# A two-block vision tower, image pairs in one merged order: the next image's patches, first attention and routing move beside the current image's second attention

## The chip, the cores and the metric

One core of a Trainium2 chip runs the whole program. The metric is the time of one execution in device microseconds, from three runs. Engine names are those of the profile: PE (TensorE's matmuls), PEld (its weight loads), DVE (VectorE), ACT (ScalarE), POOL (GpSimd), SP (SyncE, which here issues all DMAs).

## What is computed

64 images of 3 x 224 x 224 go through a patch embedding and two transformer blocks of width 192; an image has 197 tokens.

```
h = patches(x) @ W + b, class token in front, + pos_embed
h = h + softmax(q k^T / sqrt(192)) v          of layernorm(h), one head        "first attention"
h = h + w[e] * (gelu(n @ W1[e] + b1[e]) @ W2[e] + b2[e])   n = layernorm(h), e = argmax of
                                              softmax(mean over tokens of n @ Wg)   "routing", ffn 0
h = h + proj(12 heads of softmax(q k^T / 4) v) of layernorm(h)                 "second attention"
h = h + ffn of layernorm(h)                   191 patch rows: fc1, gelu, fc2   "ffn 1"
                                              6 class rows: routed pairs of five experts
```

The expert of ffn 0 is known only after the first attention of that very image, so its weights are fetched by index while the kernel runs. The six class rows of all images are done together after the loop.

## The kernel before, in words

Images are taken in pairs: p = 0 is called the **even** image here and p = 1 the **odd** one. Tokens lie as 2 tiles of 99 rows. The work on an image is cut into named stages (STAGES, line 69), and each engine has one function `stages(name, p, it)` that issues its own share of a stage and waits by semaphores. `run_stages` (line 405) lets every engine walk the same list, ORDER, once per pair: `merged_order` (line 84) makes it from the letters of MERGE (line 80), where a takes the even image's next stage, b the odd image's next one, r one regrouping step of the patches on POOL. The odd image starts B_FIRST (line 79) stages late, so the stages of one half of it belong to the pair before ("behind"); stages in AHEAD (line 68) are done for the next pair, and are run once before the loop for the first. Every engine works strictly through its share of this list.

The stages are, in the order of one image: `x` (28 transposes of regrouped pixels, for both images, copies by DVE and ACT), `tok0/1` (patch matmuls), `statN/normN/turnN` (layernorm N: moments on DVE, the power on POOL, the scaling on DVE, four transposes on PE, a copy on ACT and two remainders on DVE), `q0 v0 s0 p0 o0` (first attention: folded query-key product, values, scores, transposed weights, output), `route` (sum over tokens on DVE, PE, then seven small DVE operations and one exponential; then the loads of the expert's weights on SP, line 473), `hid0_* out0_*` (ffn 0), `qk1_* v1` (queries, keys, values), `max0` to `max5` (scores of two heads each, whose maxima DVE takes), `maxT` (the maxima turned into rows of the operand stacks by two DMAs, line 507), `att0` to `att13` (scores with the maximum in them, exponentials on ACT; every fourth head the products with the values, then shuffle, reciprocal and product on DVE: a "head group"), `proj`, layernorm 4, `hid1_* out1_*` (ffn 1).

Queries and keys as high and low parts are put into the operand stacks `q_stack` and `k_stack` by eight DMAs per image on SP, after `qk1_0` and `qk1_1`. `k_stack` lies in the tile `shared` (line 171), which at another time holds W1 of the expert. The matmuls stand in helpers: line 640 (`accumulate`), 664 (layernorm transposes), 687 and 689 (`hid_out`), 706 (`x`), 740 (`p0`), 786 (`max`), 792 (`maxT`), 804 and 817 (`att`). On DVE: 943, 948, 955 (layernorm), 965 (`x`), 981 (`turn`), 1014 to 1031 (`route`), 1035 (`out0_1`), 1041 (`qk1`), 1050 (`max`), 1059 to 1063 (head group). Each image has four PSUM banks; TURN_BANK and HIDDEN_BANK (lines 106 and 107) say which stages use which.

In ORDER before, the even image's `max0` to `att2` stand with no stage of the odd image between them; the odd image's `max0` to `att2` have the even image's layernorm 4 and ffn 1 between them. The first attention of each image stands beside the other's late second attention, layernorm 4 and ffn 1, and is followed by routing and, 14 to 16 places later in the merged order, by ffn 0. Layernorm 1 of the next pair is made a pair ahead (`x`, `tok`, layernorm 1 only are in AHEAD).

Of the kernel before, what the change touches and what calls it, by code (L numbers as in the profile page):

```python
# [17 lines left out]
ALU = mybir.AluOpType  # L18
# [6 lines left out]
D = 192  # L25
# [21 lines left out]
RING = 6  # L47
STAGED = 2
# [12 lines left out]
def ffn_stages(n):  # L61
# [6 lines left out]
AHEAD = ["x", "tok0", "tok1"] + norm_stages(1)  # L68
STAGES = (["q0", "v0", "s0", "p0", "o0"] + norm_stages(2)
          + ["route", "x", "tok0", "tok1", "stat1", "split", "norm1", "hid0_0", "hid0_1", "turn1",  # L70
             "hid0_2", "out0_0", "out0_1"] + norm_stages(3) + ["qk1_0", "qk1_1", "qk1_2", "v1"]
          + [("max", j) for j in range(HEADS // 2)] + ["maxT"] + [("att", s) for s in range(HEADS + 2)]
          + ["proj"] + norm_stages(4) + ffn_stages(1))

B_FIRST = 38
MERGE = ("bbbbbabbabbbbabbababbbabaababbbababaaabbaaabababararbaabrbabbbaabrbbarabbrbaaaaa"  # L80
         "aaabaababaaaabaababaaabaaabbabbrabbabaabbab")
# [24 lines left out]
TURN_BANK = {1: 3, 2: 3, 3: 0, 4: 1}  # L106
# [3 lines left out]
def vit_kernel(nc, x, tok_w, tok_b, cls_tok, pos, attn_w, wg, w1, b1, w2, b2, w_qkv, w_proj, b_proj,  # L110
               fc1_w, fc1_b, fc2_w, fc2_b, gate_pair, atom_in_w, atom_in_b, atom_out_w, atom_out_b,
               balance, out, scratch):
    with ExitStack() as ctx:
# [52 lines left out]
        with ExitStack() as loop:  # L166
# [13 lines left out]
            w2_sb = two("w2_sb", [128, HC, D])  # L180
# [50 lines left out]
            probs0 = [probs[p][0][:, 0, :, :] for p in range(2)]  # L231
            turned = [probs[p][0][:, 1, :, :] for p in range(2)]
            y = two("y", [R, T, D])
# [164 lines left out]
        def norm_count(n, it):  # L398

            if n == 1:  # L400
                return 1 if isinstance(it, int) and it == 0 else 4 * it - 1
            last = isinstance(it, int) and it == PAIRS - 1
            return 4 * it + {2: 2, 3: 4 - last, 4: 5 - last}[n]
# [27 lines left out]
        def _(sp):  # L431
# [36 lines left out]
            def stages(name, p, it):  # L468
# [4 lines left out]
                if name == "route":  # L473

                    sp.wait_ge(expert_ready[p], it + 1)
# [44 lines left out]
                if name == "out1_1":  # L520
# [3 lines left out]
                                 y[p][NCLS - 1:R - 1, 0, :]).then_inc(stored[p], 16)  # L524
                    sp.dma_start(out[bass.ds(img, 1), R:SEQ].rearrange("o s d -> (o s) d"),
                                 y[p][0:R - 1, 1, :]).then_inc(stored[p], 16)
# [66 lines left out]
        def _(pe):  # L593
# [82 lines left out]
            def hidden(p, n, j, chunk):  # L676
                for c in (2 * j, 2 * j + 1):
                    last = accumulate(bank[p][HIDDEN_BANK[n][j]][:, (c % 2) * SP_:(c % 2 + 1) * SP_],
                                      swapped(products(tokens(p), chunk(c))))
                last.then_inc(hid_done[p], 1)  # L680
# [585 lines left out]
```

## Time and profile before

| | us |
|---|---|
| runs | 4169.99, 4172.8, 4182.94 (median 4172.8) |
| the profiled execution | 4169.49 |
| its span, first to last instruction | 4167.7 |
| PE busy | 3189.7 |
| DVE busy | 2134.8 |
| ACT busy | 1402.9 |
| POOL busy | 360.5 |

The mean granted clock of TensorE over the span is 0.862. The loop over pairs starts at some 67 us and PE leaves it at 4044 us; behind it come the class rows. An instruction row of the trace gives its start in us from the span's start, its length, engine, line and operation, output and inputs, shapes, how many were merged, and in brackets how long its engine sat idle before it and what ended that.

### The profile page before, as it was taken

Reading aid. Unit: us, or ns where it says so; the run is one execution under the profiler, and the core shown is the slowest. Engines: PE = TensorE matmul, PEld = TensorE weight load, DVE = VectorE, ACT = ScalarE, POOL = GpSimd, SP = SyncE. Lnnn points to the kernel's source line nnn. Section 1 sums busy time; section 2 is a strip of 40 time slices with the busy share of each in tenths; the row PEclk is TensorE's granted clock in tenths of the full one; section 3 lists DMA queues with packets and bytes.
Section 4 is the critical chain, followed back from the end, with each engine's and each line's share of the span. In section 5 each row is a group of like instructions: output and inputs, shape, how many; then the busy total and the mean of one; then the engine's idle time right before and its main releaser. Section 6 shows DMA issues by size and latency. Waiting matters only on the chain.

```text
span 4167.7 us, 63512 instructions
## 1 busy us (share of the span) xinstructions
PE 3189.7 (77%) x23190; PEld 2834.1 (68%) x23190; DVE 2134.8 (51%) x5288; ACT 1402.9 (34%) x2904; POOL 360.5 (9%) x746
## 2 busy tenths in 40 slices
PE   4777877777877777777777787777778777777757
PEld 3667766767766676776666776667677666677646
DVE  4555555554555555555555455554555555555433
ACT  2333333333333333333333333333333333333321
POOL 1000000010000000010001000010010000100000
PEclk9888888888988888888888898888888888889877
DMA  4332222332322333222233232223322223322221
GB/s 122 79 80 70 69 60 47 81 79 69 79 57 56 64 79 78 71 70 58 47 81 79 69 81 66 55 54 80 80 69 73 56 47 80 79 73 66 64 62 32
DMA packets 127223, 287.54 MB, mean 69 GB/s; under 512 B 28791, under 2 KB 95368, under 8 KB 116173
## 3 DMA queue, kind: packets, MB, share of 16 engines
q1 hardware_dynamic: 127180, 286.97, 29.7%
q8 instruction: 27, 0.44, 0.0%
q14 instruction: 16, 0.12, 0.0%
HBM read 192.23 MB, written 15.00 MB: 50 GB/s over the span
## 4 chain that ended last, share of the span: by engine, by line
PE 47%; DVE 29%; DMA 8%; issue 5%; SPq 4%; ACT 4%; POOL 3%; DVEq 0%; POOLq 0%; ACTq 0%
PE banks L640 21%; PE banks L687 8%; DVE inv L1061 5%; DVE hx L955 5%; PE banks L817 5%; DMA shared<-low 4%; DVE nmax L1050 4%; PE banks L786 4%; PE banks L804 3%; DMA shared<-nmaxT 3%; DVE stats L943 3%; POOL rstd L586 2%; PE banks L664 2%; DVE xnT L981 2%; DVE sums L1059 2%
## 5 line engine op out<-in xcount | busy, mean ns | idle before, releaser
L786 PE MATMUL banks<-shared,q_stack 128*99 128x198 f32 x1536 | 282.2, 336 | 238.4 <-issue 103.3
L1050 DVE TENSOR_REDUCE nmax<-banks 99x4 f32<-99x788 f32 x384 | 360.3, 974 | 155.8 <-PE banks L786 152.5
L786 PEld LDWEIGHTS banks<-shared,q_stack 128*99 128x99 f32 x1536 | 225.3, 225 | 292.3 <-issue 110.8
L640 PE MATMUL banks<-xnT,fc_wT 128*128 128x198 f32 x1920 | 359.3, 363 | 42.1 <-DVE xnT L981 42.1
L640 PEld LDWEIGHTS banks<-xnT,fc_wT 128*128 128x128 f32 x1920 | 346.0, 278 | 50.1 <-DVE xnT L981 50.0
L804 PE MATMUL banks<-q_stack,shared 128*99 128x198 f32 x1536 | 268.0, 301 | 140.1 <-DMA shared<-nmaxT 118.4
L1191 ACT ACTIVATE xnT<-banks 128x396 fp32r<-128x396 f32 x192 | 96.1, 501 | 820.6 <-PE banks L664 820.6
L584 POOL TENSOR_TENSOR var_eps<-moments,eps 99x2 f32<-99x2 f32 x256 | 51.1, 200 | 3642.2 <-DVE moments L948 3642.2
L804 PEld LDWEIGHTS banks<-q_stack,shared 128*99 128x99 f32 x1536 | 204.4, 194 | 203.6 <-DMA shared<-nmaxT 106.8
L687 PE MATMUL banks<-w_sb,hidT 128*99 128x192 f32 x1536 | 338.7, 383 | 0.0
L955 DVE TENSOR_SCALAR hx<-hx,moments,rstd 99x192 f32<-99x192 f32 (+1 forms) x768 | 248.0, 385 | 160.8 <-POOL rstd L586 157.2
L1226 ACT ACTIVATE probs_first<-banks 99x396 f32<-99x396 f32 x256 | 114.0, 497 | 616.2 <-PE banks L804 616.2
L687 PEld LDWEIGHTS banks<-w_sb,hidT 128*99 128x99 f32 x1536 | 293.2, 201 | 11.7
L687 PE MATMUL banks<-fc_wT,hidT 128*99 128x192 f32 x1536 | 273.0, 327 | 0.0
L640 PE MATMUL banks<-tok_wT,xT 128*99 128x192 f32 x1536 | 270.0, 330 | 3.5 <-ACT xT L1182 0.9
L1061 DVE RECIPROCAL inv<-sums 128x198 f32<-128x198 f32 x192 | 267.2, 1392 | 6.6
L817 PE MATMUL banks<-probs_rest,vals 99*32 99x198 f32 (+1 forms) x2048 | 186.7, 361 | 100.4 <-DVE headT L1063 65.5
L640 PEld LDWEIGHTS banks<-tok_wT,xT 128*99 128x99 f32 x1536 | 245.4, 168 | 8.9 <-issue 7.2
L1226 ACT ACTIVATE probs_rest<-banks 99x396 f32<-99x396 f32 x512 | 228.0, 497 | 64.6 <-PE banks L804 61.3
L687 PEld LDWEIGHTS banks<-fc_wT,hidT 128*99 128x99 f32 x1536 | 240.6, 166 | 0.5
L1209 ACT ACTIVATE hidT<-banks,fc_bc 128x198 f32<-128x198 f32 x384 | 142.5, 423 | 290.3 <-PE banks L640 290.3
L664 PE MATMUL banks<-ident,hx 99*128 99x99 f32 x1024 | 158.0, 284 | 106.2 <-DVE hx L955 103.9
(191 smaller groups left out, 5592.3 us busy)
## 6 DMA issues: line engine op xcount, KB each, us to landing
shared<-w_split SPq DMA_DIRECT2D x64, 1188.0 KB
xin<-in_x_dram SPq DMA_DIRECT2D x32, 1176.0 KB
w_sb<-in_L_ffn_W_dram SPq DMA_DIRECT2D x64, 576.0 KB, 6.2
w_last<-w_split SPq DMA_DIRECT2D x64, 384.0 KB
q_stack<-hi SPq DMA_DIRECT2D x128, 148.5 KB
q_stack<-low SPq DMA_DIRECT2D x128, 148.5 KB
shared<-hi SPq DMA_DIRECT2D x128, 148.5 KB
shared<-low SPq DMA_DIRECT2D x128, 148.5 KB
```

What stands on the lines that cost most here:

```text
L640: last = t_.matmul(dst, a, b, start=(j == 0), stop=(j == len(pairs) - 1))
L664: last = t_.transpose(b[:, k * SP_ + t * R:k * SP_ + (t + 1) * R], xn[p][:, t, k * 128:(k + 1) * 128], ident[0:R, 0:R])
L687: t_.matmul(b[0:R, t * D:(t + 1) * D], hidT[p][:, c, t * R:(t + 1) * R], w[:, c, :], start=(c == 0), stop=False)
L786: last = t_.matmul(b[n % 4][0:R, t * SP_:(t + 1) * SP_], q_stack[p][:, n, t * R:(t + 1) * R], k_stack[p][:, n, :], start=True, stop=True)
L804: last = t_.matmul(b[s % 2][0:R, kt * SP_:(kt + 1) * SP_], k_stack[p][:, s, kt * R:(kt + 1) * R], q_stack[p][:, s, :], start=True, stop=True)
L817: last = t_.matmul(b[2][r:r + 32, 0:SP_], vals[p][0:rows, kt, head(h), :], ring(p, h)[0:rows, kt, :], start=(kt == 0), stop=(kt == T - 1))
L943: last = v.bn_stats(stats[p][:, t, :], (h_tok[p] if n == 1 else h_tiles[p])[:, t, :])
L955: last = v.tensor_scalar(xn[p][:, t, at:at + D - lo], (h_tok[p] if n == 1 else h_tiles[p])[:, t, lo:D], moments[p][:, t, 0:1], rstd[p][:, ...
L1050: v.tensor_reduce(nmax1[p][:, :, 2 * j:2 * j + 2].rearrange("p t h -> p h t"), src, AX, ALU.max, negate=True).then_inc(nmax1_ready[p], 1)
L1061: v.reciprocal(inv1[p][:], sums1[p][:]).then_inc(inv1_ready[p], 1)
L1209: last = s_.activation(hidT[p][:, c, :], b[HIDDEN_BANK[layer][j]][:, (c % 2) * SP_:(c % 2 + 1) * SP_], ACT.Gelu, bias=bias[:, c:c + 1], sc ...
L1226: s_.activation(ring(p, s).rearrange("p k s -> p (k s)"), b[s % 2][0:R, 0:T * SP_], ACT.Exp).then_inc(p1_ready[p], 1)
```

## The change

What it does: AHEAD now reaches from `x` to `route` and a new stage `load` (the expert's DMAs, which so far stood in `route`): all of that is done for the next pair. In STAGES the first attention, layernorm 2 and routing of the next image stand between the `att` stages of the same image's second attention (BESIDE says behind which), `x`, `tok` and layernorm 1 stand between layernorm 3 and `v1`, `q0` and `v0` before `max0`, `load` behind `proj`. B_FIRST and MERGE are other values. For this, buffers no longer shared: `vals0`, `probs0` and `turned` get tiles of their own (laid over `w2_sb`'s place, see the diff), the first attention keeps its result in `h_tok`, `y` goes and the output is stored from `h`. Banks: the first attention uses bank 3 (before: 0 to 3) and `v0` bank 1; layernorm 4 turns into `tokT`. `load` waits for `proj` of the image before, whose keys lie in `shared`. The kinds, shapes and numbers of the instructions of each stage stay, but for `p0` and `o0`, which take 98 keys in the second tile where it took 99.

The order after, from one `max0` of the even image to the next (E even, O odd, +1 the next pair's image):

```
E.max0 O.turn4 E.max1 E.max2 O.hid1_0 O.hid1_1 E.max3 O.hid1_2 E.max4 E.max5 O.out1_0 O.out1_1
O.hid0_0 O.hid0_1 E.maxT O.hid0_2 O.out0_0
E.att0 E.s0+1 E.att1 O.out0_1 E.att2 E.p0+1 O.stat3 E.att3 E.att4 E.o0+1 O.norm3 E.stat2+1
E.att5 E.att6 E.att7 O.tok0+1 E.norm2+1 E.att8 O.tok1+1 O.turn3 E.att9 E.att10 E.att11 E.att12 E.turn2+1
O.qk1_0 E.att13 O.qk1_1 O.v1 O.stat1+1 E.route+1 O.norm1+1 E.proj E.load+1 O.turn1+1 E.stat4
O.q0+1 E.norm4 O.v0+1
O.max0 O.max1 E.turn4 O.max2 O.max3 E.hid1_0 O.max4 O.max5 E.hid1_1 O.maxT E.hid1_2 E.out1_0
O.att0 O.s0+1 O.att1 E.out1_1 O.att2 E.hid0_0 O.p0+1 E.hid0_1 E.hid0_2 E.out0_0 E.out0_1 E.stat3
O.att3 O.att4 O.o0+1 E.x+1 O.stat2+1 O.att5 O.att6 O.att7 O.norm2+1 E.norm3 E.tok0+1 O.att8 O.att9
O.att10 E.tok1+1 O.att11 E.turn3 O.att12 O.turn2+1 O.att13
E.qk1_0 E.qk1_1 E.v1 E.stat1+1 O.route+1 E.norm1+1 O.proj O.load+1 E.turn1+1 O.stat4 E.q0+1 E.v0+1 O.norm4
```

The diff, cut to its core:

```diff
-AHEAD = ["x", "tok0", "tok1"] + norm_stages(1)
-STAGES = (["q0", "v0", "s0", "p0", "o0"] + norm_stages(2)
...
+AHEAD = (["x", "tok0", "tok1"] + norm_stages(1) + ["q0", "v0", "s0", "p0", "o0"] + norm_stages(2)
+         + ["route", "load"])
+BESIDE = {0: ["s0"], 2: ["p0"], 4: ["o0", "stat2"], 7: ["norm2"], 12: ["turn2"], 13: ["route"]}
+ATTENTION = []
+for s in range(HEADS + 2):
+    ATTENTION += [("att", s)] + BESIDE.get(s, [])
+STAGES = (ffn_stages(0) + ["stat3", "x", "norm3", "tok0", "tok1", "turn3", "qk1_0", "qk1_1", "v1"]
+          + norm_stages(1) + ["q0", "v0"] + [("max", j) for j in range(HEADS // 2)] + ["maxT"] + ATTENTION
+          + ["proj", "load"] + norm_stages(4) + ffn_stages(1))
...
-B_FIRST = 38
+B_FIRST = 30
...
-TURN_BANK = {1: 3, 2: 3, 3: 0, 4: 1}
+TURN_BANK = {1: 0, 2: 3, 3: 1, 4: 1}
...
-            w2_sb = two("w2_sb", [128, HC, D])
+            w2_sb, vals0, probs0, turned = [], [], [], []
+            for p in range(2):
+                with ExitStack() as weights:
+                    w2_sb.append(sb(f"w2_sb{p}", [128, HC, D], stack=weights))
+                vals0.append(sb(f"vals0{p}", [R, T, D], stack=loop))
+                probs0.append(sb(f"probs0{p}", [R, T, SP_], stack=loop))
+                turned.append(sb(f"turned{p}", [R, T, SP_], stack=loop))
...
-            y = two("y", [R, T, D])
...
+        def norm_source(p, n):
+            return h_tok[p] if n <= 2 else h_tiles[p]
+
+        def turned_tile(p, n):
+            return (xnT if n in (2, 3) else tokT)[p]
...
-                if name == "route":
+                if name == "load":
+                    if not isinstance(it, int) or it:
+                        sp.wait_ge(proj_done[p], it)
+                        sp.nop(nofuse=True)
                     sp.wait_ge(expert_ready[p], it + 1)
...
-                    if not isinstance(it, int) or it:
-                        pe.wait_ge(logit_ready[0], it)
...
                 elif name == "q0":
                     pe.wait_ge(xnT_ready[p], norm_count(1, it))
+                    if not isinstance(it, int) or it:
+                        pe.wait_ge(v_ready[p], 2 * it)
...
                 elif name == "v0":
                     if not isinstance(it, int) or it:
-                        pe.wait_ge(out_ready[p], it)
-                    values(p, it, b[3], attn_wv, tokT)
+                        pe.wait_ge(low_ready[p], 2 * it - 1)
+                    values(p, it, b[1], attn_wv, tokT)
...
-                        if not (isinstance(it, int) and it == PAIRS - 1):
-                            pe.wait_ge(xnT_ready[p], norm_count(1, it + 1))
+                        if isinstance(it, int) and it == 0:
+                            pe.wait_ge(logit_ready[p], 1)
+                        else:
+                            pe.wait_ge(out_ready[p], it)
...
-                        pe.wait_ge(v_ready[p], 2 * it + 2)
+                        if isinstance(it, int) and it == PAIRS - 1:
+                            pe.wait_ge(v_ready[p], 2 * it + 2)
+                        else:
+                            pe.wait_ge(v_ready[p], 2 * it + 3)
+                            pe.wait_ge(g_ready[p], it + 2)
...
+                    if name == "out1_0" and not (isinstance(it, int) and it == PAIRS - 1):
+                        pe.wait_ge(logit_ready[p], it + 2)
...
+                if not (n == 1 and isinstance(it, int) and it == 0):
+                    dve.wait_ge(xn_turned[p], norm_count(n, it) - 1)
...
-                    v.scalar_tensor_tensor(out=h[p], in0=b[3][0:R, 0:T * D], scalar=weight[p][:, 0:1], in1=h[p],
+                    dve.wait_ge(stored[p], 32 * it + 32)
+                    v.scalar_tensor_tensor(out=h[p], in0=b[3][0:R, 0:T * D], scalar=weight[p][:, 0:1],
+                                           in1=h_tok[p][:].rearrange("p t d -> p (t d)"),
```

## Rows read from the trace of the kernel before

**Rows 1.** Stretches: us, busy by engine (x instructions), granted clock, DMA share, GB/s.

```profile
1965.00:2088.00 123.00, 95.86 (x722) 85.80 (x720) 65.04 (x163) 43.39 (x90) 11.12 (x23) 0.88 0.30 71
...
2009.00:2019.80 10.80, 5.32 (x26) 4.06 (x26) 7.65 (x15) 0.00 (x0) 0.88 (x2) 0.59 0.01 2
...
2037.00:2050.00 13.00, 9.62 (x67) 8.87 (x68) 8.61 (x17) 4.09 (x9) 1.44 (x3) 0.87 0.05 7
```

**Rows 2.** PE in order of time: first and last `x` inside the loop.

```profile
116.56 1.18 PE L706 MATMUL banks<-ident,xg 84*128 84x84 f32 x14
...
3807.52 1.18 PE L706 MATMUL banks<-ident,xg 84*128 84x84 f32 x14
```

**Rows 3.** PE in order of time: the even image's second attention.

```profile
2009.25 0.98 PE L786 MATMUL banks<-shared,q_stack 128*99 128x198 f32 x8 [3.24 <-DMA shared<-low]
...
2019.91 0.99 PE L804 MATMUL banks<-q_stack,shared 128*99 128x198 f32 x4 [3.38 <-DMA shared<-nmaxT]
...
2034.00 1.22 PE L640 MATMUL banks<-proj_wT,headT 128*99 128x192 f32 x6 [1.36 <-DVE headT L1063]
```

**Rows 4.** PE in order of time: the odd image's second attention, from `qk1_0`.

```profile
2025.21 1.09 PE L640 MATMUL banks<-xnT,qk_wT 128*96 128x198 f32 x10
...
2039.28 0.98 PE L786 MATMUL banks<-shared,q_stack 128*99 128x198 f32 x8 [2.91 <-issue]
...
2065.65 1.22 PE L640 MATMUL banks<-proj_wT,headT 128*99 128x192 f32 x6 [1.32 <-DVE headT L1063]
```

**Rows 5.** PE in order of time: the rest of the pair.

```profile
2070.20 1.54 PE L640 MATMUL banks<-vals,probs_first 99*99 99x192 f32 x8 [1.84 <-DVE probs_first L997]
...
2073.74 6.16 PE L640 MATMUL banks<-xnT,fc_wT 128*128 128x198 f32 x30 [1.31 <-DVE xnT L981]
...
2117.70 2.10 PE L640 MATMUL banks<-xnT,qk_wT 128*96 128x198 f32 x20 [1.31 <-DVE xnT L981]
```

**Rows 6.** PE in order of time: 12 matmuls of `out1_0` and of `out0_0`.

```profile
2080.08 2.12 PE L687 MATMUL banks<-fc_wT,hidT 128*99 128x192 f32 x12
...
2104.93 4.16 PE L687 MATMUL banks<-w_sb,hidT 128*99 128x192 f32 x12
```

**Rows 7.** DVE in order of time: layernorm 3, head group, remainder, routing.

```profile
2016.85 0.60 DVE L943 BATCH_NORM_STATS2 stats<-hx 99x6 f32<-99x192 f32 x2
...
2018.88 1.11 DVE L955 TENSOR_SCALAR hx<-hx,moments,rstd 99x192 f32<-99x192 f32 x4 [1.08 <-POOL rstd L586]
...
2025.01 0.39 DVE L1059 STREAM_SHUFFLE sums<-banks 128x198 f32<-128x198 f32 x1
...
2026.86 0.37 DVE L1063 TENSOR_TENSOR headT<-banks,inv 128x198 f32<-128x198 f32 x1
...
2027.14 0.55 DVE L1041 SCALAR_TENSOR_TENSOR low<-hi,banks 96x396 fp32r<-96x396 f32 x1
...
2081.83 0.57 DVE L1014 TENSOR_REDUCE xsum<-banks 128x2 f32<-128x394 f32 x1
...
2084.16 0.16 DVE L1031 TENSOR_TENSOR weight<-ltop,linv 99x1 f32<-99x1 f32 x1
```

**Rows 8.** SP in order of time: first and last of the five loads of an expert.

```profile
2106.79 0.38 SPq L483 DMA_DIRECT2D shared<-w_split  x1
...
2108.95 0.34 SPq L489 DMA_DIRECT2D w_sb<-in_L_ffn_W_dram  x1
```

**Rows 9.** The page: DMA queue (packets, MB, share) and the last load (us to landing).

```profile
q1 hardware_dynamic: 127180, 286.97, 29.7%
...
w_sb<-in_L_ffn_W_dram SPq DMA_DIRECT2D x64, 576.0 KB, 6.2
```

**Rows 10.** PE in order of time before the loop: `q0` of the even, then of the odd image.

```profile
93.84 2.44 PE L640 MATMUL banks<-tokT,qk_fold 128*128 128x198 f32 x10
...
112.70 2.45 PE L640 MATMUL banks<-tokT,qk_fold 128*128 128x198 f32 x10
```

**Rows 11.** PE in order of time: the last matmul of the loop.

```profile
4043.43 0.39 PE L689 MATMUL banks<-bias_pair,ones_pair 128*99 128x192 f32 x1
```

More of the change, by code:

```diff
@@ L47 @@
 RING = 6
+ROUTED = 448
 STAGED = 2
@@ L62, in ffn_stages @@
     return [f"hid{n}_0", f"hid{n}_1", f"hid{n}_2", f"out{n}_0", f"out{n}_1"]
-AHEAD = ["x", "tok0", "tok1"] + norm_stages(1)
-STAGES = (["q0", "v0", "s0", "p0", "o0"] + norm_stages(2)
[L70 to L73, printed above, removed]
-B_FIRST = 38
-MERGE = ("bbbbbabbabbbbabbababbbabaababbbababaaabbaaabababararbaabrbabbbaabrbbarabbrbaaaaa"
-         "aaabaababaaaabaababaaabaaabbabbrabbabaabbab")
+AHEAD = (["x", "tok0", "tok1"] + norm_stages(1) + ["q0", "v0", "s0", "p0", "o0"] + norm_stages(2)
[8 more added lines that the diff above has]
+B_FIRST = 30
+MERGE = ("abaaaaabbbabbbbbarabbbababbbaaaababbabaababraabbabaabbbbabbaaabaarbabaabaaaabaab"
+         "barraaaabarbbbabaabababrbbabbabbabaabbbab")
 def merged_order():
@@ L737, in stages @@
                     pe.wait_ge(p0_ready[p], it + 1)
[L738 removed]
+                    for kt, keys in ((0, R), (1, SEQ - R)):
                         for t in range(T):
[L740 to L741 removed]
+                            last = t_.transpose(b[3][0:keys, kt * SP_ + t * R:kt * SP_ + (t + 1) * R],
+                                                probs0[p][:, t, kt * R:kt * R + keys], ident[0:R, 0:R])
                     last.then_inc(p0_turned[p], 1)
@@ L746, in stages @@
                     for t in range(T):
-                        last = accumulate(b[2][0:R, t * D:(t + 1) * D],
-                                          [(turned[p][:, kt, t * R:(t + 1) * R], vals[p][:, kt, :, 0:HD])
-                                           for kt in range(T)])
+                        last = accumulate(b[3][0:R, t * D:(t + 1) * D],
+                                          [(turned[p][0:keys, kt, t * R:(t + 1) * R], vals0[p][0:keys, kt, :])
+                                           for kt, keys in ((0, R), (1, SEQ - R))])
                     last.then_inc(o0_done[p], 1)
@@ L1002, in stages @@
                     dve.wait_ge(inv0_ready[p], it + 1)
-                    if not (isinstance(it, int) and it == 0):
-                        dve.wait_ge(out_ready[p], it)
-                    dve.wait_ge(cls_stored[p], 32 * it + 32)
                     for t in range(T):
-                        last = v.scalar_tensor_tensor(out=h_tiles[p][:, t, :], in0=b[2][0:R, t * D:(t + 1) * D],
+                        last = v.scalar_tensor_tensor(out=h_tok[p][:, t, :], in0=b[3][0:R, t * D:(t + 1) * D],
                                                       scalar=inv0[p][:, t:t + 1], in1=h_tok[p][:, t, :],
```

60 lines of the change are left out of this document (29 added, 31 removed).

## The prediction

> **What bounds the kernel now.** I read the page first, whose busy times stand in the table above: PE works 3190 of 4168 us, DVE 2135, ACT 1403, and the 40 slices look alike but for the last few, so one pair of images stands for the loop. The first and the last `x` inside the loop are 3690.96 us and 30 pairs apart [rows 2]: **123.03 us per pair**. The windows view of one pair [rows 1] says that PE is busy for 95.86 of 123 us, so it idles 27.1 us, and that the granted clock is 0.88: for 24% of the time, some 29.5 us, it has the lower of its two levels. No other engine comes near: DVE is busy 65 us, ACT 43. So a pair costs PE's work plus the waits of PE, which walks its stages in a fixed order, and the waits are what to look for.
>
> The timeline of PE shows them in its brackets. They come in three kinds, and each sum below is over all brackets of one pair.
> - The even image's maxima. From `max0` to `att0` nothing of the other image stands in the order. PE works 5.3 of 10.8 us at a clock of 0.59 [rows 1], and waits 3.38 us for the maxima's DMAs at the end [rows 3]. The odd image's same stretch has layernorm 4 and ffn 1 of the even one in it. There PE is busy 9.6 of 13 us, and 2.3 of the 3.4 idle us are the end of the wait before `max0` [rows 1, 4].
> - The wait of `max0` for the operand stacks: 3.24 and 2.91 us [rows 3, 4]. From `qk1_0` to `max0` it is 14.07 us in the odd image [rows 4] and 14.1 in the even one, whatever stands between, so this is the length of the chain of eight DMAs.
> - Single waits for DVE: `proj` for the last head group, 1.36 and 1.32 [rows 3, 4]; `o0`, and whatever follows a layernorm, 1.84, 1.31 and 1.31 [rows 5]; in all some 16 us with the small ones.
>
> **The change, part by part.** The stages keep their instructions, so PE's, DVE's and ACT's work stays (PE 95.9 us at today's clocks). What changes is what stands beside what.
>
> *Even maxima.* The stretch now holds the odd image's `turn4`, ffn 1 and ffn 0 up to `out0_0`, more than the odd stretch of before. I take 1.2 us of idle time, the odd stretch's 3.4 less its 2.3 for the stacks, where there were 5.5: **-4.3**. Bounds: 0 and 5.5.
>
> *Odd maxima.* The fillers stay `turn4`, `hid1` and `out1_0`. But DVE now comes to layernorm 4 only after routing, layernorm 1 and `q0`'s remainder, so `turn4` and the first maxima are late: I take 2.9 instead of 1.2: **+1.7**. Bounds: 1.1 and 5.5.
>
> *From `qk1_0` to `max0`, both images.* This stretch is new and the weak place of the order. After the last head group's matmuls (`att13`), PE has `qk1_1` and `v1`, 2.0 us in all, while DVE has, in its order, `turn2`'s remainders or a first `qk1` remainder (about 0.6), the head group 2.2, the `qk1_1` remainder 0.55, the moments of layernorm 1 0.95 and the sum over tokens 0.57 [rows 7], 4.9 us, before PE may do `route`: 2.9 us of idle time. From the end of that sum to the routing weight it is 1.9 us, then the four scalings 1.1 [rows 7]; `route` and `proj` (0.6 + 2.4) cover it but for 0.1. `q0` then follows its own transposes at once: 1.3, as such a wait costs today [rows 5]. `max0` waits for ACT's copy of `v0`: 0.6. That is 4.9 us per image, 9.8 per pair, and the stacks' 14.1 us end no later than this chain, which is some 14 to 16 us long. In the even image's attention `att13` also waits for the head group before, which DVE does after layernorm 3 and `tok1` of the other image, 1.3, and `qk1_0` 0.35. The waits that go: 6.15 for the stacks, 4.8 of `att13` and `proj` around the last head groups (1.36 and 1.32 of it are in [rows 3, 4]). So 11.5 where 11.0 were: **+0.5**. Bounds: 7 (the stacks alone, less what the other waits give) and 20 (every Vector item a layernorm later).
>
> *The first attention and the layernorms elsewhere.* `s0`, `p0`, `o0` now have `att` stages and another image's ffn between them, each 1.6 us or more where the wait was 1.84; layernorms 2 and 3 have 5 us and more of such work behind their moments. Today's rest is 27.1 less 5.5, 1.2 and 11.0, so 9.4 us. It shrinks to some 1.6: `x`'s own copies 0.3, exponentials 0.8, a head group 0.5, all three as today. **-7.8**. Bounds: 1 and 6 us left.
>
> Sum of idle time: -4.3 + 1.7 + 0.5 - 7.8 = **-9.9 us**, 17.2 left.
>
> *Clock.* The same 12 matmuls take 4.16 us at the lower level and 2.12 at the higher [rows 6]. The clock is low where idle time is dense, as at the even maxima [rows 1]. With a third of the idle time gone, and most of what is left around `route` and `q0`, I take 24 us at the lower level instead of 29.5; PE loses a third to a half of such time, so **-2.0**. Bounds: +3 and -9.
>
> *Loads.* `load` is on SP behind the eight stack DMAs of the other image and ahead of its `maxT`. An expert takes from 2106.79 to 6.2 us after 2108.95, 8.4 us [rows 8, 9]. It is issued when `proj` is done, just before `max0`; first use, `hid0_0`, is 12 us of PE time behind `max0` in the odd image and further in the even one: hidden. Without that cover each image would wait up to 8.4 us.
>
> *Waits added.* On DVE `out0_1` waits for the stored output of the same image, whose stores are issued a whole ffn 0 earlier, some 9 us; behind it on DVE stand `p0`'s copy and the other moments, so if the stores were late, `o0` and `att9` would be. On PE `out0_0` waits for DVE's `out1_1`, three `hid0` stages earlier, and `max0` for `q0`'s remainder and `v0`'s copy, priced above. On SP `load` waits for `proj`; behind it stand only the class rows' stores and `maxT`. The scalings' wait for the transposes before is over long before. All 0 but what is priced.
>
> *ACT and POOL.* From exponential to gelu and back ACT now changes 6 times per pair, not 8; ACT is 65% idle, so 0. The Trainium skill (ScalarE: Activation LUTs, What ACT_TABLE_LOAD costs) puts a change at about 2.66 us with its drain, so its sum would be 5.3 us of ACT time less per pair; on PE's path it would be nothing either unless ACT bounds. POOL's two powers per layernorm and its seven copies stay.
>
> So a pair takes 123.0 - 9.9 - 2.0 = **111.1 us**.
>
> *The ends.* Before the loop the first attention of both images now runs alone. From `q0` of the even image to that of the odd one, behind its routing, it is 18.9 us [rows 10]. The even image is ready for its `q0` at 84, so done at 103; the odd one needs 13 for its patches and layernorm 1 and again 18.9, so 135; ffn 0 of the even image 9 more: the first `x` in the loop at 144 instead of 116.6. Behind the last `x` there were 236 us to the end of the loop [rows 2, 11]; now 101 to the end of that pass (`x` stands some 10 us behind its beginning), 90 for the last pass (111 less the 21 us of PE work of a first attention that is no longer there), 32 for the odd image's last half as now: 223. The class rows keep 124 us.
>
> Sum: 144 + 30 x 111.1 + 223 + 124 = 3824 us of span. The profiled execution was 1.8 us over its span, and the median of the runs another 3.3 over it: **3830 us**, 8.2% less. Within 0.3% (12 us) a measurement of this kernel can't tell it from no change.
>
> **The rivals.**
> 1. *DVE's order becomes the bound.* Its 65 us come in a row wherever two layernorms, a head group and routing meet. If each of the two stretches before `max0` and each attention costs 2 us more than worked out, a pair takes 119 us and the kernel 4075. For it: every one of these items is in line ahead of `route`. Against: DVE is idle 40% of such a pair.
> 2. *The clock stays up.* If the lower level nearly goes, -9 instead of -2: 104 us per pair, 3610. Against: some 17 us of idle time remain, in two clumps.
> 3. *Slower: the loads delay the maxima's DMAs.* Nearly everything goes through one queue, q1 [rows 9], and `maxT`'s two DMAs now stand behind five loads of 2.1 MB. In my order they follow 13 us after the first load, which needs 8.4 [rows 8, 9] once the stacks are through. If stacks and loads slip so that maxima and `hid0` wait, each us beyond a slack of some 5 is paid per image; from 6 us per image on the gain is eaten, and at 7 a pair takes 125 and the kernel 4255. The Trainium skill (DMA: Bandwidth & Descriptors, Queues, rings and completion order) says that an engine takes a queue's descriptors in the order of its ring; the trace agrees as far as nothing but one queue carries data. Against: the DMA engines are busy 30% [rows 1].
> 4. *No change:* the new chain before `max0` costs what the maxima gave, 123 per pair, 4170.
>
> **How the numbers follow.** My forecast, with its own range of 3720 to 3960 (108 to 115.5 us per pair), gets 0.58; rival 1 (3960 to 4150) 0.17, rival 2 (under 3720) 0.12, rival 3 (over 4190) 0.10, rival 4 0.03. Faster: 0.58 + 0.17 + 0.12 = 0.87; same 0.03; slower 0.10. The range takes in the forecast and most of rivals 1 and 2, and leaves out rivals 3 and 4 and the far ends of 1 and 2: 3650 to 4090.
>
> **What would show it.** Right: `x` every 111 us; the even image's `att0` with less than 1 us before it; the longest brackets of PE at `route` (about 3 us, for DVE's sum) and at `q0` (1.3, for the remainder); no wait for `load` at `hid0_0`. Wrong: long brackets at `max0` for a DMA (the stacks, not DVE, end last), at `att0` or `hid0_0` for a DMA (rival 3), at `att13` and `turn` stages for DVE (rival 1), or a granted clock below 0.85.

## The result and the profile after

The changed kernel takes **3446.9 us** (median of 4 runs, 3436.1 to 3450.4) where before takes 4174.8 us (4 runs): a ratio of **0.825**, 95% interval 0.8228 to 0.8273. The forecast was 3830 us, range 3650 to 4090: the direction was right, and the gain is twice the forecast's. The profiled execution took 3436.1 us, 1.8 us over its span.

PE in order of time, the first and the last `x` inside the loop and the last matmul of the loop, as in [rows 2, 11]:

```profile
143.60 1.18 PE L721 MATMUL banks<-ident,xg 84*128 84x84 f32 x14
...
3097.42 1.18 PE L721 MATMUL banks<-ident,xg 84*128 84x84 f32 x14
...
3311.33 0.39 PE L706 MATMUL banks<-bias_pair,ones_pair 128*99 128x192 f32 x1
```

Thirty pairs lie between the two `x`: **98.46 us per pair** instead of 123.03. That is 737 us of the 733 gained; the ends cancel (27 us more ahead of the loop, 22 and 1.3 us less behind it).

The windows view, 2000 us in the middle of the loop, before:

```profile
1000.00:3000.00 2000.00, 1558.25 (x11497) 1391.26 (x11495) 1047.90 (x2612) 693.53 (x1439) 181.65 (x376) 0.87 0.30 69
```

And after, the same stretch, the even image's maxima from `max0` to `att0`, and the odd image's, as in [rows 1]:

```profile
1000.00:3000.00 2000.00, 1755.49 (x14363) 1611.65 (x14362) 1235.60 (x3247) 838.73 (x1769) 221.53 (x464) 0.95 0.39 86
1939.40:1956.80 17.40, 16.58 (x130) 15.81 (x130) 7.93 (x14) 7.51 (x15) 0.00 (x0) 1.00 0.29 111
1987.00:1999.70 12.70, 11.46 (x91) 10.41 (x92) 7.57 (x13) 5.79 (x10) 0.00 (x0) 1.00 0.28 111
```

PE's share rises from 77.9 to 87.8%. Times the pair: 95.9 us of work and 27.2 idle before, **86.4 and 12.0 after**. So a pair loses 15.1 us of idle time, and 9.4 us of PE's own work although its instructions are the same. The granted clock says most of why (the rest stands in the account below): 0.87 is 26% of the time at the lower level (32 us of a pair), 0.95 is 10% (10 us). The even maxima, at 0.59 before, run at 1.00.

Which work became shorter is read from the groups of PE's matmuls (count, busy us, mean ns, idle us ahead of them). Before:

```profile
L640 PE MATMUL banks<-xnT,fc_wT 128*128 128x198 f32 x1920 | 359.3, 363 | 42.1 <-DVE xnT L981 42.1
L687 PE MATMUL banks<-w_sb,hidT 128*99 128x192 f32 x1536 | 338.7, 383 | 0.0
L786 PE MATMUL banks<-shared,q_stack 128*99 128x198 f32 x1536 | 282.2, 336 | 238.4 <-issue 103.3 <-DMA shared<-low 95.2 <-DVE nmax L1050 36.2
...
L640 PE MATMUL banks<-proj_wT,headT 128*99 128x192 f32 x768 | 148.2, 336 | 87.1 <-DVE headT L1063 87.1
```

After, the same groups (`hid1`, `out0`, the maxima, `proj`):

```profile
L656 PE MATMUL banks<-tokT,fc_wT 128*128 128x198 f32 x1920 | 281.2, 302 | 5.1 <-DVE tokT L1007 5.0
...
L704 PE MATMUL banks<-w_sb,hidT 128*99 128x192 f32 x1536 | 268.1, 326 | 0.0
...
L809 PE MATMUL banks<-shared,q_stack 128*99 128x198 f32 x1536 | 233.2, 290 | 91.2 <-DMA shared<-low 32.2 <-ACT vals L1220 25.6 <-DVE nmax L1075 18.1
...
L656 PE MATMUL banks<-proj_wT,headT 128*99 128x192 f32 x768 | 200.8, 417 | 2.9 <-DVE headT L1088 2.9
```

Three groups together give back 198 us. `proj` got slower, 336 to 417 ns: it now follows PE's longest wait in the loop, that of `route`. The timeline of one pair after shows that, and the largest waits that are left:

```profile
1956.73 0.42 PE L827 MATMUL banks<-q_stack,shared 128*99 128x198 f32 x2 [0.28 <-DMA shared<-nmaxT]
...
1972.68 0.88 PE L840 MATMUL banks<-probs_rest,vals 99*32 99x198 f32 x16 [0.76 <-DVE headT L1088]
...
1977.80 0.60 PE L656 MATMUL banks<-wgT,xsum 128*99 128x3 f32 x4 [2.23 <-DVE xsum L1037]
1978.32 1.66 PE L656 MATMUL banks<-proj_wT,headT 128*99 128x192 f32 x6
...
1979.94 2.13 PE L656 MATMUL banks<-proj_wT,headT 128*99 128x192 f32 x6
...
1984.02 1.36 PE L656 MATMUL banks<-tokT,qk_fold 128*128 128x198 f32 x10 [1.32 <-DVE tokT L1007]
...
1987.06 0.96 PE L809 MATMUL banks<-shared,q_stack 128*99 128x198 f32 x8 [0.78 <-ACT vals L1220]
...
2028.38 1.22 PE L656 MATMUL banks<-proj_wT,headT 128*99 128x192 f32 x6
```

The even `att0` waits 0.28 us (3.38 in [rows 3]). The largest brackets left are those of `att13`, `route`, `q0` and `max0`, as the forecast said. Six `proj` matmuls take 1.66 and 2.13 us behind the even `route`, and six take 1.22 behind the odd one in this pair: the granted clock is 0.54 from 1979.9 to 1982.6 us, nearly all of it the lower level, and 1.00 from 2028.3 to 2031.4.

Below, idle time and PE's own work per pair are sums of the gaps and of the rest, over the same 22 pairs of each trace, from the starts and ends of PE's rows; added matmuls count as idle time.

### The profile page after: what moved, and what is told of

Read it like the earlier page. It is cut to its first block, busy times and chain, and to the rows that moved or that the text cites. A ratio compares the mean times of both kernels' runs of the same rounds, so it can differ in the third digit from the quotient of the medians.

```text
span 3434.3 us, 64029 instructions
## 1 busy us (share of the span) xinstructions
PE 2907.5 (85%) x23190; PEld 2647.5 (77%) x23190; DVE 2032.5 (59%) x5286; ACT 1347.6 (39%) x2840; POOL 356.6 (10%) x746
## 4 chain that ended last, share of the span: by engine, by line
PE 46%; DVE 30%; DMA 9%; issue 6%; SPq 5%; ACT 3%; DVEq 0%; POOL 0%; POOLq 0%; ACTq 0%
PE banks L656 24%; PE banks L704 11%; DVE inv L1086 7%; DVE hx L981 5%; PE banks L809 4%; DMA shared<-low 4%; DMA shared<-nmaxT 4%; DVE nmax L1075 3%; DVE stats L967 2%; PE banks L827 2%; DVE sums L1084 2%; DVE xnT L1007 2%; SPq L525 2%; PE banks L680 1%; DVE low L1066 1%
## 5 line engine op out<-in xcount | busy, mean ns | idle before, releaser
L809 PE MATMUL banks<-shared,q_stack 128*99 128x198 f32 x1536 | 233.2, 290 | 91.2 <-DMA shared<-low 32.2
L656 PE MATMUL banks<-tokT,fc_wT 128*128 128x198 f32 x1920 | 281.2, 302 | 5.1 <-DVE tokT L1007 5.0
L656 PEld LDWEIGHTS banks<-tokT,fc_wT 128*128 128x128 f32 x1920 | 260.8, 216 | 14.3 <-DVE tokT L1007 14.1
L704 PE MATMUL banks<-w_sb,hidT 128*99 128x192 f32 x1536 | 268.1, 326 | 0.0
L704 PEld LDWEIGHTS banks<-w_sb,hidT 128*99 128x99 f32 x1536 | 241.1, 166 | 0.0
L656 PE MATMUL banks<-xnT,shared 128*128 128x198 f32 x1536 | 229.0, 280 | 0.0
L1234 ACT ACTIVATE hidT<-banks,b_sb 128x198 f32<-128x198 f32 x384 | 142.3, 422 | 215.3 <-PE banks L656 214.1
L656 PEld LDWEIGHTS banks<-xnT,shared 128*128 128x128 f32 x1536 | 205.7, 195 | 0.0
L656 PE MATMUL banks<-proj_wT,headT 128*99 128x192 f32 x768 | 200.8, 417 | 2.9 <-DVE headT L1088 2.9
L1216 ACT ACTIVATE tokT<-banks 128x396 fp32r<-128x396 f32 x128 | 64.0, 500 | 353.8 <-PE banks L680 353.8
```

The lines of the kernel that those rows point to most:

```text
L656: last = t_.matmul(dst, a, b, start=(j == 0), stop=(j == len(pairs) - 1))
L704: t_.matmul(b[0:R, t * D:(t + 1) * D], hidT[p][:, c, t * R:(t + 1) * R], w[:, c, :], start=(c == 0), stop=False)
L809: last = t_.matmul(b[n % 4][0:R, t * SP_:(t + 1) * SP_], q_stack[p][:, n, t * R:(t + 1) * R], k_stack[p][:, n, :], start=True, stop=True)
L1234: last = s_.activation(hidT[p][:, c, :], b[HIDDEN_BANK[layer][j]][:, (c % 2) * SP_:(c % 2 + 1) * SP_], ACT.Gelu, bias=bias[:, c:c + 1], sc ...
```

## The experiments

Two theories were to be told apart. **A:** PE's clock is a cost of its own, about as large as a third of the gain, and it depends on where the idle time lies. **B:** the change gained by filling PE's waits alone, and the clock is only a sign of that. And the two parts of the change were to be priced: the even maxima's cover, and the first attention's new place.

| kernel | us | ratio to before (95%) | us per pair | idle | PE's own work |
|---|---|---|---|---|---|
| before | 4174.8 | 1 | 122.9 | 27.2 | 95.7 |
| after | 3446.9 | 0.825 (0.8228 to 0.8273) | 98.7 | 12.1 | 86.6 |
| even maxima bare | 3807.4 | 0.9129 (0.911 to 0.9149) | 110.6 | 19.4 | 91.2 |
| bare, PE kept at work | 3699.0 | 0.8854 (0.8838 to 0.887) | 107.2 | 19.3 | 87.9 |
| first attention apart | 3870.6 | 0.9273 (0.9257 to 0.9288) | 112.6 | 18.9 | 93.7 |
| `route` later | 3449.4 | 0.8264 (0.8249 to 0.828) | 99.0 | 11.0 | 88.0 |
| `route` later, PE kept at work | 3364.6 | 0.8067 (0.8052 to 0.8082) | 95.9 | 13.4 | 82.6 |
| after, PE kept at work at two waits | 3411.8 | 0.8183 (0.8167 to 0.8198) | 97.7 | 13.4 | 84.3 |
| after, at three waits | 3378.7 | 0.8091 (0.8077 to 0.8104) | 96.9 | 13.6 | 83.4 |
| before, PE kept at work at its maxima | 4168.1 | 0.9994 (0.9984 to 1.0003) | 123.0 | 28.0 | 95.0 |
| before, at every wait | 4017.3 | 0.9636 (0.9613 to 0.9658) | 118.4 | 30.5 | 87.9 |
| before, at every wait, half as many | 3944.4 | 0.9439 (0.9423 to 0.9454) | 115.7 | 28.7 | 87.1 |

**The parts of the change.** *Even maxima bare:* in after's order, the odd image's `turn4`, ffn 1 and ffn 0 are moved ahead of the even `max0` (O odd, E even; `...` stands for stages that keep their order).

```diff
-E.max0 O.turn4 E.max1 E.max2 O.hid1_0 ... O.out0_0 E.att0
+O.turn4 O.hid1_0 ... O.out0_0 E.max0 E.max1 ... E.maxT E.att0
```

> The kernel after, with the even image's max0 to att0 standing bare as in the kernel before: the odd image's turn4, ffn 1 and ffn 0 come ahead of them instead of between them. Theory (cover and clock both count): PE idles 5 us more in that stretch, 1 less at max0, and the clock falls there as it did before: +7 to +9 us per pair, 3680 to 3740 us. Rival (the waits alone): +3.8 us per pair, 3570 us.

It took 3807.4 us, 11.9 us more per pair than after: more than expected, since 4.6 of it are PE's own work. The idle time is 7.3 us more, 5.5 of it in the bare stretch; the view of PE's waits (total us, times, longest) shows the old wait for the maxima's DMAs again, and behind it after's row for that wait:

```profile
PE banks L827 <- DMA shared<-nmaxT: 120.1, 64, 3.5
```

```profile
PE banks L827 <- DMA shared<-nmaxT: 19.1, 64, 0.3
```

The theory's mechanism holds, but its sum was too small: it booked 7 to 9 us for waits and clock together, where the waits alone cost 7.3. The rival falls.

*First attention apart:* the first attention, layernorm 2 and the routing follow `att13` instead of standing between the own image's `att` stages; the even maxima's cover stays. B_FIRST and MERGE change with it, so that these stages stand in turn with the other image's `qk1_*`, `v1` and layernorm 1.

```diff
-    ATTENTION += [("att", s)] + BESIDE.get(s, [])
+    ATTENTION += [("att", s)]
...
-          + ["proj", "load"] + norm_stages(4)
+          + ["s0", "p0", "o0", "stat2", "proj", "norm2", "turn2", "route", "load"] + norm_stages(4)
```

> The kernel after, but the first attention, layernorm 2 and the routing no longer stand between the own image's `att` stages: they follow `att13`, in turn with the other image's `qk1`, `v1` and layernorm 1. The cover of the even maxima stays as after. Theory (their place beside the second attention is worth about what the forecast booked for it, 7.8 us of idle time per pair, and the clock adds about half as much again): 108 to 112 us per pair where after has 98.7, so 3750 to 3860 us. Rival (the cover of the maxima alone gave the gain, and the first attention is covered anywhere): within 2% of after, 3380 to 3520.

3870.6 us, 10 above the theory's range; the rival falls. Idle time rose by 6.8 us, PE's own work by 7.1. The waits view shows single waits for DVE and ACT:

```profile
PE banks L680 <- DVE hx L981: 232.7, 191, 5.2
...
PE banks L757 <- ACT probs L1176: 94.8, 64, 1.8
```

After has 3.2 us in 2 times for the second. Its row for the first, and before's:

```profile
PE banks L680 <- DVE hx L981: 25.4, 7, 5.2
```

```profile
PE banks L664 <- DVE hx L955: 103.9, 125, 5.1
```

So this order waits more for the scalings than before did. It isn't the first attention's old place either: in ORDER before only the even image's first attention stands beside the other image's second attention, and the odd one's has the even image's patches, layernorm 1 and ffn 0 beside it. The prices of the two parts, 361 and 424 us, make 784 against 728 for the whole. The first is the price of leaving the even maxima bare as in before. The second is the price of this one order; what before's own place cost is not shown apart.

**The clock in after.** Matmuls were added ahead of waits, with constant operands and into a bank that is free at that place.

```diff
+            def fill(b, n):
+                for _ in range(n):
+                    t_.matmul(b[:, 0:SP_], qk_wT[:, 0, 0, 0:128], qk_wT[:, 0, 0, 0:SP_], start=True, stop=True)
...
                 elif name == "q0":
+                    fill(bank[1 - p][1], 8)
...
                 elif name == "route":
+                    fill(b[0], 14)
```

> The kernel after, with 14 such fillers ahead of route and 8 ahead of q0, where its two largest waits of PE are (2.2 and 1.3 us per image). Theory (clock): what is left of the lower level, some 7 us per pair, mostly goes; 1.5 to 2.5 us per pair, about 3385 us, -1.8%. Rival (waits only): 3447 within 0.5%, or slower by the fillers' overrun.

3411.8 us: a gain of 35 us where 62 were expected; the rival falls too. PE's own work fell by 2.3 us, but the idle time rose by 1.3: the even image's wait before `max0` grew from 1.0 to 2.2 us (means of the 22 pairs). The stacks' DMAs set its end, so part of what PE saves ahead of it is waited for there. The third wait, ahead of `max0`:

```diff
                     if j == 0:
+                        fill(bank[1 - p][1], 7)
                         pe.wait_ge(low_ready[p], 2 * it + 2)
```

> The kernel after with added matmuls whose results are never read: 14 ahead of each `route` and 8 ahead of each `q0`, as in the run before, and now 7 ahead of each `max0` too, where PE waits 0.8 and 1.0 us for the values' copy and the operand stacks. Theory (what is left of the lower level comes from idle time just ahead of the maxima): clock 0.96 to 0.98, another 20 to 40 us off 3412, so about 3380. Rival (what is left lies elsewhere, or the added matmuls delay `max0`): 3400 to 3430.

3378.7 us, as the theory had it. PE's own work is 83.4 us, 3.2 less than after's; the even image's wait before `max0` is still 2.2 us, now with the seven matmuls in it.

*`route` later:* the sum over tokens, which `route` waits 2.2 us for, becomes a stage of its own (`xsum`) at the place on DVE where `route` stood, and PE does `proj` and the other image's `turn1` ahead of `route`. AHEAD, MERGE and DVE's part of the two stages change with it.

```diff
-BESIDE = {... 12: ["turn2"], 13: ["route"]}
+BESIDE = {... 12: ["turn2"], 13: ["xsum"]}
...
-          + ["proj", "load"] + norm_stages(4) ...
+          + ["proj", "route", "load"] + norm_stages(4) ...
```

> The kernel after, with routing split: DVE's sum over tokens right behind the moments of layernorm 1 (while POOL works), proj ahead of route, and route's matmuls and its seven DVE operations behind turn1. Theory (DVE's chain from the last head group to turn1 sets max0 in the even-to-odd half, the eight stack DMAs, 14.1 us from qk1_0, in the other): 1.7 us and 0.5 us less, some 2.2 per pair, about 3380 us, and max0 waits for the stacks in both halves. Rival (DVE's chain sets both): 2.4 us per image, 3300 us. Rival 2 (routing's place does not matter): 3447.

3449.4 us, the time of after (0.8264 against 0.825, the intervals overlap). The stretch from `qk1_0` to `max0` did get shorter, as the theory had it: 14.4 instead of 14.7 us in the even image and 14.3 instead of 15.8 in the odd one (means of the 22 pairs), some 1.8 us per pair of the 2.2 expected. Idle time fell by 1.1 us, but PE's own work rose by 1.4. The windows view (0.91 where after has 0.95) and the groups show what happened to the clock:

```profile
1000.00:3000.00 2000.00, 1777.36 (x14278) 1652.59 (x14279) 1235.81 (x3248) 832.99 (x1760) 220.91 (x463) 0.91 0.38 85
```

```profile
L656 PE MATMUL banks<-tokT,fc_wT 128*128 128x198 f32 x1920 | 333.6, 340 | 1.3 <-DVE tokT L1007 1.3
...
L809 PE MATMUL banks<-shared,q_stack 128*99 128x198 f32 x1536 | 266.1, 327 | 120.2 <-DMA shared<-low 86.5 <-DVE nmax L1076 17.5 <-issue 15.3
...
L656 PE MATMUL banks<-proj_wT,headT 128*99 128x192 f32 x768 | 145.7, 333 | 16.4 <-DVE headT L1089 16.4
```

`proj`, ahead of the wait now, is back to 333 ns; the maxima and `hid1`, behind the waits of `turn1`, `q0` and `max0` that now stand close together, went from 290 to 327 and from 302 to 340. *With PE kept at work* at those three:

```diff
                     n = int(name[4])
+                    if n == 1:
+                        fill(bank[1 - p][1], 10)
...
                 elif name == "q0":
+                    fill(bank[1 - p][1], 8)
...
                     if j == 0:
+                        fill(bank[1 - p][1], 10)
```

> The kernel with `route` moved behind `turn1` (idle time 11.0 us per pair instead of 12.1, yet the same time as after, at a mean granted clock of 0.900), with matmuls added whose results are never read: 10 ahead of each `turn1`, 8 ahead of each `q0`, 10 ahead of each `max0`, about 1 us each time, where PE waits 1.0 to 1.7 us. Theory (what that move gained in idle time was given back by the lower clock in the hidden layer and the maxima behind the waits): clock over 0.94, PE's own work back to about 85.6 us per pair from 88.0, 96.5 us per pair, about 3375 us, faster than after with its fillers (3412). Rival (the added matmuls only fill or lengthen the waits, and the chain through the stacks sets the time): 3410 to 3460.

**3364.6 us, the fastest of all**, 2.4% under after by its median; the rival falls. The same groups, and the windows view of the loop:

```profile
L656 PE MATMUL banks<-tokT,fc_wT 128*128 128x198 f32 x1920 | 267.3, 292 | 1.3 <-DVE tokT L1015 1.3
...
L817 PE MATMUL banks<-shared,q_stack 128*99 128x198 f32 x1536 | 219.5, 274 | 116.4 <-DMA shared<-low 64.6 <-DVE nmax L1084 28.7 <-issue 21.0
...
L656 PE MATMUL banks<-proj_wT,headT 128*99 128x192 f32 x768 | 145.8, 333 | 16.4 <-DVE headT L1097 16.4
```

```profile
1000.00:3000.00 2000.00, 1855.14 (x15987) 1714.63 (x15985) 1283.23 (x3373) 860.15 (x1819) 231.11 (x483) 1.00 0.40 88
```

The clock is 1.00, PE's own work 82.6 us, 5.4 less than without the added matmuls. So what the move had gained, the lower clock behind the waits had taken back. What the move itself is worth is better read between the two kernels with added matmuls, where the clock is at 0.99 or more in both: 14 us, 0.4% (3378.7 to 3364.6), with intervals that overlap a little. The same with the even maxima bare, with matmuls added ahead of the waits that this brings:

```diff
                     n = int(name[4])
+                    if n == 4 and p == 1:
+                        fill(bank[0][0], 10)
...
                     if j >= 2:
+                        if p == 0:
+                            fill(bank[1][2], 2)
...
                 elif name == "maxT":
+                    if p == 0:
+                        fill(bank[1][2], 8)
...
                         if s == 0:
+                            if p == 0:
+                                fill(bank[1][2], 26)
...
                 elif name[:4] == "hid1":
+                    if name == "hid1_0" and p == 1:
+                        fill(bank[0][0], 10)
```

> The kernel with the even maxima bare again (3807 us, 110.6 us per pair; against after 7.3 us more idle time and 4.6 us more of PE's own work at the lower clock), with matmuls added whose results are never read where PE waits there: 10 ahead of the odd image's `turn4` and of its `hid1_0`, 2 ahead of `max2` to `max5`, 8 ahead of `maxT`, 26 ahead of `att0`. Theory (the 4.6 us are the clock's, and come back when PE is kept at work): clock 0.93 or more, 106 to 107 us per pair, 3660 to 3690 us. Rival (as in before with its fillers, the matmuls that run at the lower level do so where a wait for a DMA follows, so that nothing is gained): 3780 to 3820.

3699.0 us: the idle time is the same (19.3), PE's own work 87.9 instead of 91.2, so 3.3 of the 4.6 us came back; 9 us short of the theory's range, far from the rival's.

**The clock in before.** First the maxima alone, where the clock is lowest [rows 1]:

```diff
+                        fill(bank[1][2] if p == 0 else bank[0][1], 14)
                         pe.wait_ge(low_ready[p], 2 * it + 2)
...
+                        if p == 0:
+                            fill(bank[1][2], 4)
                         pe.wait_ge(nmax1_ready[p], 6 * it + j - 1)
...
+                            if p == 0:
+                                fill(bank[1][2], 14)
                             pe.wait_ge(nmaxT_ready[p], it + 1)
```

> The kernel before, with filler matmuls (constant operands, results never read, 0.11 us each at the higher clock) put into three waits of PE: 14 ahead of each image's max0, 14 ahead of the even image's att0, 4 ahead of each of its max2 to max5. The order and all waits stay. Theory (an idle gap costs PE twice, by the wait and by the lower clock behind it): granted clock from 0.86 to 0.92 or more, PE's own stages 4 to 5 us per pair shorter, about 4030 us, -3.5%. Rival (only the waits count, low-clock work falls beside waits anyway): within 0.5% of before, or up to 1% slower where a filler overruns its wait.

4168.1 us, no change: the theory as put falls. Its groups say where it was wrong:

```profile
L687 PE MATMUL banks<-w_sb,hidT 128*99 128x192 f32 x1536 | 337.6, 383 | 0.0
L640 PE MATMUL banks<-xnT,fc_wT 128*128 128x198 f32 x1920 | 330.3, 342 | 42.1 <-DVE xnT L990 42.1
...
L793 PE MATMUL banks<-shared,q_stack 128*99 128x198 f32 x1536 | 257.5, 314 | 126.4 <-issue 68.1 <-DMA shared<-low 49.8 <-DVE nmax L1059 8.1
```

`out0` stayed at 383 ns and `hid1` came from 363 to 342 only: they are dense work behind other waits (those for layernorms and head groups, [rows 5]), which this run left empty. The maxima went from 336 to 314 ns, but what PE saves there it waits for, since the chain through DVE and the DMAs sets their end: its own work fell by 0.7 us per pair and its idle time rose by 0.8. So next the same ahead of every wait of about 1 us or more, all as above:

> The kernel before, with matmuls whose results are never read (114 ns each at the higher level) ahead of every wait of PE of about 1 us or more: 26 ahead of each `max0`, 4 ahead of the even `max2` to `max5`, 8 ahead of the even `maxT`, 28 ahead of the even `att0`, 11 ahead of each `proj`, 8 ahead of each `att13`, 15 ahead of the even `o0`, 11 ahead of the odd `hid1_0`, 10 ahead of the even `turn1` and of the odd `turn2`, 11 ahead of the even `qk1_0`. The first such run had them at the maxima alone: PE's own work went from 95.7 to 95.0 us per pair, and the odd `hid1_0` (2.46 us) and the even `out0_0` (4.21 us) behind the other waits stayed at the lower level. Theory (the clock is a cost of its own, which the idle time ahead of dense work brings, and not a sign of it): PE's own work 87 to 89 us, the waits as they are, 114.5 to 117 us per pair, 3920 to 4000 us, so that 5% could be had in the order of before. Rival (in before the work at the lower level is hidden behind the chains that set the waits): above 4100 us.

4017.3 us, 3.6% faster than before: the rival falls. PE's own work is 87.9 us as the theory had it, but the time is 17 us over its range. The waits view has a line that before has not (it is at the odd image's `att3`), and the page's line of the queue of instructions (packets, MB, share) is another than before's `27, 0.44, 0.0%`:

```profile
PE banks L821 <- issue: 57.7, 28, 2.8
```

```profile
q8 instruction: 291, 4.77, 0.6%
```

So the added matmuls were made twice as wide and half as many, 102 per pair instead of 199:

```diff
-                for _ in range(n):
-                    t_.matmul(b[:, 0:SP_], qk_wT[:, 0, 0, 0:128], qk_wT[:, 0, 0, 0:SP_], start=True, stop=True)
+                for _ in range((n + 1) // 2):
+                    t_.matmul(b[:, 0:384], qk_wT[:, 0, 0, 0:128], qk_wT[:, 0, 0, 0:384], start=True, stop=True)
```

> The run before (4017 us; PE's own work 87.9 us per pair as the theory of the clock had it, waits 30.5 instead of 27.2) had a new wait of 2.06 us in 28 passes, at the odd `att3`, which ends on nothing that the profile shows, 57.7 us in all, and its queue of instructions carried 291 packets, 4.77 MB, where before has 27 and 0.44 MB. Here the added matmuls have 384 columns instead of 198 and are half as many, so that PE is kept at work for about the same time with half the added instructions. Theory (the new wait is PE fetching instructions, since the added matmuls made the loop's body longer): the queue of instructions back to some 30 packets, the wait at `att3` gone, 3950 to 3975 us. Rival (the wait has to do with the work itself, such as exponentials that are now late): 4000 to 4030 us, the wait still there.

3944.4 us, 6 us better than the theory's range; the wait is gone, and the queue's line is:

```profile
q8 instruction: 30, 0.49, 0.1%
```

Its groups, and the windows view:

```profile
L687 PE MATMUL banks<-w_sb,hidT 128*99 128x192 f32 x1536 | 299.1, 353 | 0.0
...
L640 PE MATMUL banks<-xnT,fc_wT 128*128 128x198 f32 x1920 | 250.6, 284 | 7.6 <-DVE xnT L1003 7.6
```

```profile
1000.00:3000.00 2000.00, 1813.63 (x14013) 1610.20 (x14013) 1112.36 (x2781) 742.47 (x1542) 190.43 (x394) 0.99 0.31 72
```

In before's own order, with all its waits left (28.7 us idle), the clock alone is worth **230 us, 5.6%**. So the clock is a cost of its own, as A says, and B falls; how much of the change's gain is the clock stands in the next section.

## Why the prediction was right or wrong

**The step that failed is the price of PE's own work: -2.0 us per pair in the clock's term, nothing elsewhere; it is -9.4.** The idle time alone would not have left the range: with the measured -15.1 and the forecast's -2.0 the forecast's sum gives 105.9 us per pair and some 3670 us. With -9.4 and the forecast's idle time it gives some 3610, outside.

*The time at the lower level.* The forecast scaled it with the idle time (24 us instead of 29.5). The windows show 32 us before and 10 after. What was wrong is what it follows. It isn't proportional to idle time: `route` later has the least idle time of the kernels without added matmuls (11.0 us) and a worse clock than after, and before with 28.7 us, filled, has 0.99. The runs show it to go with which dense work stands behind bare waits. The change took the bare waits away ahead of `hid1`, `out0` and the maxima, and left one ahead of `proj`.

*What that time costs.* Where only matmuls were added ahead of waits, PE's own work fell by 8.6 us for some 29 us less at the lower level (before), 3.2 for 8.5 (after), 5.4 for 16 (`route` later): 0.3 to 0.4 of it, near the lower end of "a third to a half". Of the 22 us that the change takes away, some 6 lay in PE's idle time, where there is no work to slow down. The Trainium skill (TensorE: Matmul & The Clock Gate, HAM oscillation — how this bites in real kernels) counts half of the time at the lower level as lost, which as an estimate makes 11 us of those 22; the runs show less.

*What the clock leaves over.* The 9.4 us are not the clock's alone. At the same clock, 0.99, before's order still has 87.1 us of own work and after's 83.4. The forecast had PE's work stay but for the clock; but PE stops less often after, at 19 gaps per pair instead of 30, and each stop costs more than its bracket. In a dense stretch a row's last matmul overlaps the next row, here by 0.29 us of 2.11 (the profile models where a matmul ends); ahead of a gap it does not:

```profile
1946.64 2.11 PE L704 MATMUL banks<-fc_wT,hidT 128*99 128x192 f32 x12
1948.46 0.39 PE L706 MATMUL banks<-bias_pair,ones_pair 128*99 128x192 f32 x1
```

Fitted to the twelve rows of the table (an estimate from their traces, within 0.3 us for each), PE's own work is 77.8 us, 0.43 for each us of it at the lower level (25.7 before, 9.8 after) and 0.24 for each gap. That makes some 6.9 us for the clock and 2.6 for the stops.

**The idle time was sized too carefully: -9.9 forecast, -15.1 measured.** By the forecast's own parts, per pair:

| part | before | forecast | after |
|---|---|---|---|
| even `max0` to `att0` | 5.5 | 1.2 | 0.5 |
| odd `max0` to `att0` | 1.2 | 2.9 | 1.1 |
| `qk1_0` to `max0`, both | 11.0 | 11.5 | 9.8 |
| the rest | 9.4 | 1.6 | 0.7 |

- *Even maxima:* right in kind, and the bare run prices it back (5.5 us in that stretch).
- *Odd maxima:* the late layernorm 4 that was booked doesn't show; no row of `turn4` has a wait in either half of the pair from 1936 to 2038 us.
- *The new chain:* the places and most sizes are right: `att13` 0.8 (forecast 1.3), `route` 2.2 and 2.0 (2.9), `q0` 1.3 and 1.4 (1.3), `max0` 0.8 and 1.0 (0.6). Before the even image's `max0` it is the stacks' DMA that ends last, where the forecast had it end no later than the new chain; its near tie of 14 to 16 us was right (14.7 us from the even `qk1_0` to `max0`, 15.8 in the odd image).
- *First attention and layernorms elsewhere:* -7.8 forecast, -8.7 measured; with it apart in the order above, 6.8 us of idle time return.

**The ends** were right, or nearly: the first `x` at 144 (143.6), 223 us behind the last one (214), 124 for the class rows (122.6). **Loads, waits added, ACT:** 0, as forecast. SP's rows show an expert's loads issued up to 1.5 us ahead of the even image's `max0` (1939.48), and that image's DMAs of the maxima 15.8 us behind the last of them:

```profile
1935.82 0.38 SPq L499 DMA_DIRECT2D shared<-w_split  x1
...
1937.96 0.34 SPq L505 DMA_DIRECT2D w_sb<-in_L_ffn_W_dram  x1
...
1953.71 0.85 SPq L525 DMA_DIRECT2D q_stack<-nmaxT  x1
```

No wait of PE ends on a load, so rival 3 had nothing to act on. Rival 1 (DVE's order): DVE is busy 62% of the loop, and PE waits no longer for it than the forecast said. Rival 2, that the clock stays up, is what happened. Its price of -9 is near the measured -9.4, in part by luck, since some 2.6 of these are the stops and not the clock. Its objection, that the idle time left would keep the clock low, was wrong. It gave 3610, since it kept 17 us of idle time; with 12 it is 30 x 98.46 = 2954 us, 144 ahead of them, 214 and 123 behind: the measured span of 3434.

Of the 24.6 us per pair 15.1 are waits; of the other 9.4, by the estimate above, some 6.9 are the clock (28% of the gain, where A said about a third) and 2.6 the stops. No run separates these two by itself. What also stays open: whether the odd maxima owe their 1.1 us to the order on DVE or to the higher clock; no run separates that.

## What to carry to other kernels

Price a wait of TensorE by its own length, by the overlap lost at the stop (0.24 us here), and by what the dense work behind it loses at the lower level; the last is read from the mean duration of one group of matmuls in two places of the same trace. A reordering that saves idle time can be worth nothing if it moves the waits ahead of denser work; a run with unread matmuls ahead of the waits shows how much of a kernel's time is the clock. Count what they add to the loop's instructions.

## What was not expected of the hardware

- **Instructions of a longer loop are fetched again in each pass.** Before has 708 matmuls and as many weight loads from `x` to `x` (the stretch in [rows 1] catches a few more) and 65 other instructions of PE. With 199 matmuls more, and as many weight loads, PE stood still for 57.7 us in 28 passes, and the instructions' queue carried 4.77 MB, 264 packets more than before's 27; with 102 more, 0.49 MB and no such wait. So the limit lies between 1685 and 1879 instructions of PE per pass. The Trainium skill (Runtime: NRT & Kernel Launch, Instruction fetch mechanics) gives TensorE's instruction memory 2048 instructions and calls a refill mostly hidden. The runs show the limit somewhat below that, and the 2.06 us per pass were not hidden.
- **Work that does nothing can make a kernel faster:** the 28 added matmuls per image in the fastest run, some 3 us, return 5.4 us of PE's own work per pair and cost 2.4 us more of idle time.
